# A decoder layer on one core: a new order in the opening of cross-attention, and routing with its place matmuls between wide ones

## What is computed

```
x = layernorm(x + self_attention(x))            # 32 heads of 16, causal
x = layernorm(x + cross_attention(x, context))  # 32 query heads, 8 key heads of 128, rotary
x = layernorm(x + experts(x) + shared(x))       # 16 experts of 256, the best 4 per token
scores = sigmoid(x @ gate_w.T) + bias           # the routing
topk_w, topk_idx = top_k(scores, 4)             # weights divided by their sum
out = sum over e of (silu(x Wg_e) * (x Wu_e)) * cw_e @ Wd_e + shared expert
```

## Time and profile before

| | us |
|---|---|
| median of 3 runs (1749.41 to 1754.07) | 1751.92 |
| the profiled execution | 1754.08 |
| its span | 1752.3 |
| TensorE busy | 1687.3 (96%) |
| VectorE busy | 1286.9 (73%) |
| ScalarE busy | 920.7 (53%) |
| GpSimd busy | 952.1 (54%) |

### The profile page before, as it was taken

How to read it: one execution, slowest core, us unless ns; L and a number is a source line. 1 busy time by engine, 2 the same in 40 slices (tenths; PEclk the granted TensorE clock), 3 DMA queues, 4 the chain that set the end, 5 groups by cost and what they waited for, 6 DMA issues and landing times. The chain is left out here.

```text
span 1752.3 us, 39049 instructions
## 1 busy us (share of the span) xinstructions
PE 1687.3 (96%) x15461; PEld 962.8 (55%) x15461; DVE 1286.9 (73%) x2062; ACT 920.7 (53%) x1518; POOL 952.1 (54%) x871
## 2 busy tenths in 40 slices
PE   7899999799999999999999999999889999999997
PEld 5666665455555555555555555555455555455553
DVE  6777777888888888888888888888785444344445
ACT  7676774656464645455555555565643333333334
POOL 5556664456464636465555556464634555455545
PEclk9999999999999999999999999999999999999999
DMA  5431323112212314132222132131267778877658
GB/s 164 132 86 35 79 62 81 61 57 89 69 65 73 109 43 145 44 101 93 73 74 97 37 98 71 37 109 37 82 224 217 143 147 224 242 189 150 117 97 300
DMA packets 88897, 190.68 MB, mean 109 GB/s; under 512 B 14800, under 2 KB 33744, under 8 KB 86672
## 3 DMA queue, kind: packets, MB, share of 16 engines
q1 hardware_dynamic: 65232, 130.72, 22.3%
q0 software_dynamic: 22912, 57.32, 16.1%
q10 hardware_dynamic: 576, 0.14, 0.0%
HBM read 124.95 MB, written 63.21 MB: 107 GB/s over the span
## 5 line engine op out<-in xcount | busy, mean ns | idle before, releaser
L1151 POOL TENSOR_TENSOR xa_sc<-xa_sc,xa_rs 128x1024 f32<-128x1024 f32 x32 | 60.8, 1901 | 366.4 <-DVE xa_rs L1415 366.4
L1139 POOL TENSOR_TENSOR xa_xs<-xa_xs,sn 128x512 f32<-128x512 f32 x160 | 227.8, 1424 | 52.1 <-ACT xa_xs L1221 52.1
L297 PE MATMUL bank<-xhl,front_h 128*128 128x512 f16 x640 | 244.7, 382 | 11.7 <-DVE front_l L679 9.8
L298 PE MATMUL bank<-xhl,front_h 128*128 128x512 f16 x640 | 244.5, 382 | 0.0
L299 PE MATMUL bank<-xhl,front_l 128*128 128x512 f16 x640 | 244.0, 381 | 0.0
L1146 POOL TENSOR_TENSOR xa_rr<-xa_x,xa_xs 128x512 f32<-128x512 f32 x156 | 232.0, 1487 | 17.9 <-DVE xa_x L1373 2.5
L297 PE MATMUL bank<-out_h,xa_oh 128*128 128x512 f16 x512 | 195.0, 381 | 12.9 <-DVE out_l L1418 5.2
L2195 POOL DMA_INDIRECT scratch_y<-raw_front,moe_to x79 | 125.3, 1585 | 149.8 <-DVE mo_zl L2249 118.6
L298 PE MATMUL bank<-out_l,xa_oh 128*128 128x512 f16 x512 | 194.7, 380 | 0.0
L299 PE MATMUL bank<-out_h,xa_ol 128*128 128x512 f16 x512 | 194.6, 380 | 0.0
L1220 ACT ACTIVATE xa_xs<-bank 64x512 f32<-64x512 f32 x160 | 95.0, 593 | 133.2 <-PE bank L299 117.7
(11 more groups left out here) (320 smaller groups left out, 4667.3 us busy)
## 6 DMA issues: line engine op xcount, KB each, us to landing
xa_rawc<-in_ew SPq DMA_DIRECT2D x32, 768.0 KB, 5.3
moe_ring<-scratch_w SPq DMA_DIRECT2D x16, 1536.0 KB, 8.8
scratch_w<-xa_chunk_h SPq DMA_DIRECT2D x32, 384.0 KB, 2.3
scratch_w<-xa_chunk_l SPq DMA_DIRECT2D x32, 384.0 KB, 3.3
raw_front<-in_xwq SPq DMA_DIRECT2D x8, 1024.0 KB, 7.9
raw_out<-in_xwo SPq DMA_DIRECT2D x8, 1024.0 KB, 5.8
scratch_y<-acc SPq DMA_DIRECT2D x6, 1024.0 KB, 6.3
acc<-in_x POOLq DMA_DIRECT2D x4, 1024.0 KB, 7.8
```

The source lines that it names most:

```text
L297: pe.matmul(out_ap, ah, bh, start=start and m == 0, stop=False)
L298: pe.matmul(out_ap, ah, bl, start=False, stop=False)
L1139: PO.mark(pool.tensor_tensor(xr, xr, sn[:, :].rearrange("p (a s) -> p a s", a=1) .to_broadcast([P, QT // S, S]), ALU.mult), f"sm{r}", st, ...
L1151: PO.mark(pool.tensor_tensor(s4, s4, rs[:, :, :].rearrange("p h (t a) -> p (h t) a", a=1) .to_broadcast([P, 16, S]), ALU.mult), "nm", st)
```

## The change

In the opening of cross-attention: on ScalarE the table of the exponential is loaded ahead by a one-element activation (`warm`), the first copies of step B and the exponentials of A go ahead of the norm. On VectorE the low parts of p go ahead of the second part of the output weights, the last part of these ahead of the low output parts, and the low half of the first chunk behind everything of step B's rotation. On TensorE the scores of step B's first half and the turned rows go ahead of the first two output tiles.

In routing: `at_col` is stored with its 83 columns innermost, so the moving operand is contiguous and VectorE's write has a step of 83 elements. w4 moves behind the fourth group, the products z1 behind `own`. The low parts zl1 are VectorE's instead of GpSimd's, behind `list`. TensorE does y0.0 and y0.1 ahead of the second half of `front(1)`; the 32 places of groups 0 to 3 stand one behind each of the 24 wide matmuls of that half, the other eight behind the last; those of groups 4 to 7 one behind each of the 12 wide matmuls of y0.2 and y0.3, the other 20 behind the last. `owners` follows. ScalarE's program in routing isn't changed, nor is SP's. The Timelines follow the programs; those of ScalarE, VectorE and TensorE that only mirror the order are left out here.

```diff
+                        act.activation(warm[:, :], eps[:, :], ACT.Exp)
+                        copies(b, 0)
+                        exponential(a, 0)
+                        copies(b, 1, ("woh",))
+                        exponential(a, 1)
                         ln.norm(act, 2, ln.DV, "sh2")
-                        exponential(a, 0)
-                        copies(b, 0)
-                        exponential(a, 1)
-                        copies(b, 1, ("woh",))
...
                         rotated_lo(b, 0)
+                        back_p_lo(b)
                         out_lo(1, 1)
-                        back_p_lo(b)
                         cosine(b, 2)
+                        rotated_lo(b, 1)
                         out_lo(2, 1)
-                        rotated_lo(b, 1)
-                        dve.wait_ge(AC.sem, AC.value("ch", a))
-                        chunk_lo().then_inc(s_first_l, 1)
                         cosine(b, 3)
                         rotated_lo(b, 2)
+                        DV.mark(out_lo(3, 1), "wol", b)
                         back_lo(b, (0, 1))
-                        DV.mark(out_lo(3, 1), "wol", b)
                         cosine(b, 4)
                         rotated_lo(b, 3)
                         back_lo(b, (2, 3))
                         value_lo(b)
                         rotated_lo(b, 4)
+                        dve.wait_ge(AC.sem, AC.value("ch", a))
+                        chunk_lo().then_inc(s_first_l, 1)
...
                         value(b, range(TQ))
+                        scores(b, 0)
+                        turned_rows(ln, b, 2)
                         back_out(b, (0, 1))
-                        turned_rows(ln, b, 2)
-                        scores(b, 0)
                         scores(b, 1)
                         back_out(b, (2, 3))
...
-            at_row, at_col = ([b(f"{w}{n}", [P, c, NR], F16) for n in range(NB)] for w, c in (("at_row", P), ("at_col", COLS)))
+            at_row = [b(f"at_row{n}", [P, P, NR], F16) for n in range(NB)]
+            at_col = [b(f"at_col{n}", [P, NR, COLS], F16) for n in range(NB)]
...
             DV = Timeline(sem("ro_dve"), [], 0,
-                          ["down", "chosen"] + quad("z", 0, IB) + ["w4", "slots"] + several("at", *range(4)) + quad("z", 1, IB)
-                          + several("at", *range(4, 8)) + ["own", "list", "tables", "to", "xl0", "xl1", "ws0", "ws1"])
-            PO = Timeline(sem("ro_pool"), [], 0, [x for q in range(2) for x in quad("zl", q, IB)])
+                          ["down", "chosen"] + quad("z", 0, IB) + ["slots"] + several("at", *range(4)) + ["w4"]
+                          + several("at", *range(4, 8)) + ["own"] + quad("z", 1, IB) + ["list"] + quad("zl", 1, IB) + ["tables", "to", "xl0", "xl1", "ws0", "ws1"])
+            PO = Timeline(sem("ro_pool"), [], 0, quad("zl", 0, IB))
...
-                low_parts(1)
...
-                        i = dve.tensor_tensor(at_col[g % NB][:, :, :], hit[g % 2][:, :, :], along(m.tok_no_h[:, ts], COLS), ALU.mult)
+                        i = dve.tensor_tensor(at_col[g % NB][:, :, :].rearrange("p n c -> p c n"), hit[g % 2][:, :, :], along(m.tok_no_h[:, ts], COLS), ALU.mult)
...
                 products(0)
-                then(dve.tensor_reduce(tot[:, :], top8[:, :, 0:TOPK], AX.X, ALU.add))
-                then(dve.tensor_scalar(tot[:, :], tot[:, :], 1e-20, None, ALU.add))
-                then(dve.reciprocal(rt[:, :], tot[:, :]))
-                DV.mark(dve.scalar_tensor_tensor(m.w4[:, :, :], top8[:, :, 0:TOPK], 1 / (WS * OS),
-                                                 rt[:, :].rearrange("p (t a) -> p t a", a=1).to_broadcast([P, NT, TOPK]),
-                                                 ALU.mult, ALU.mult), "w4", N0)
...
                 locate(0, 1, 2, 3)
-                products(1)
+                then(dve.tensor_reduce(tot[:, :], top8[:, :, 0:TOPK], AX.X, ALU.add))
+                then(dve.tensor_scalar(tot[:, :], tot[:, :], 1e-20, None, ALU.add))
+                then(dve.reciprocal(rt[:, :], tot[:, :]))
+                DV.mark(dve.scalar_tensor_tensor(m.w4[:, :, :], top8[:, :, 0:TOPK], 1 / (WS * OS),
+                                                 rt[:, :].rearrange("p (t a) -> p t a", a=1).to_broadcast([P, NT, TOPK]),
+                                                 ALU.mult, ALU.mult), "w4", N0)
                 locate(4, 5, 6, 7)
                 then(dve.tensor_scalar(past[:, :], end[:, :], m.tok_no[:, 0:1], None, ALU.is_lt))
                 then(dve.tensor_reduce(own_col[:, :], past[:, :], AX.X, ALU.add))
                 DV.mark(dve.tensor_scalar(own_h[:, :], own_col[:, :], float(NE - 1), None, ALU.min), "own", N0)
+                products(1)
                 wait(dve, PE, f"place{PLACES - 1}")
...
+                for n in range(IB):
+                    wait(dve, AC, f"zh1.{n}")
+                    DV.mark(dve.tensor_tensor(zl[1][:, n, :], z[:, n, :], zh[1][:, n, :], ALU.subtract), f"zl1.{n}", N0)
...
+                def place(g, n):
+                    if n == 0:
                         wait(pe, DV, f"at{g}")
+                    j, t = g * NR // NT, (g * NR + n) % NT
+                    mm = pe.matmul(bank[0][:, j * COLS:(j + 1) * COLS], at_row[g % NB][:, :, n], at_col[g % NB][:, n, :],
+                                   start=t == 0, stop=t == NT - 1, skip_group_check=True)
+                    if n == NR - 1:
                         PE.mark(mm, f"place{g}", N0)
 
...
+                def places(groups, first, last):
+                    for m in range(first, min(last, NR * len(groups))):
+                        place(groups[m // NR], m % NR)
+                def front_with_places(q, n, groups):
+                    wait(pe, DV, f"z{q - 1}.{n}")
+                    tok, m = slice(q * QT, (q + 1) * QT), 0
+                    for u in range(2):
+                        c, o = u * FI + n * P, bank[2 + 2 * n + u]
+                        for k in range(KD):
+                            h, l = wf_h[:, k, c:c + P], wf_l[:, k, c:c + P]
+                            for w, x in ((h, xh), (l, xh), (h, xl)):
+                                mm = pe.matmul(o[:, :], w, x[:, k, tok], start=k == 0 and w is h and x is xh,
+                                               stop=k == KD - 1 and x is xl, skip_group_check=True)
+                                m += 1
+                                if m == 6 * KD:
+                                    PE.mark(mm, f"gu{q}.{n}", N0)
+                                places(groups, m - 1, m)
+                    places(groups, m, 4 * NR)
+                def back(q, *ts, groups=()):
                     if q == 0:
                         wait(pe, DV, "down")
-                    wait(pe, PO, f"zl{q}.1")
+                    wait(pe, DV if q else PO, f"zl{q}.1")
+                    m = 0
                     for t in ts:
                         if t >= 2:
                             wait(pe, AC, f"y{q}.{t - 2}")
                         elif q:
                             wait(pe, AC, f"y{q - 1}.{t + 2}")
                         tok = slice(t * P, (t + 1) * P)
-                        PE.mark(three_pass(pe, bank[6 + t % 2][:, :], [(zh[q % 2][:, n, tok], zl[q % 2][:, n, tok], wo_h[:, n, :], wo_l[:, n, :])
-                                                                       for n in range(IB)]), f"y{q}.{t}", N0)
+                        for n in range(IB):
+                            for a, w in ((zh, wo_h), (zh, wo_l), (zl, wo_h)):
+                                mm = pe.matmul(bank[6 + t % 2][:, :], a[q % 2][:, n, tok], w[:, n, :], start=n == 0 and a is zh and w is wo_h,
+                                               stop=n == IB - 1 and a is zl, skip_group_check=True)
+                                m += 1
+                                if m % (3 * IB) == 0:
+                                    PE.mark(mm, f"y{q}.{t}", N0)
+                                places(groups, m - 1, m)
+                    places(groups, m, 4 * NR)
...
-                front(1)
-                place_picks(0, 1, 2, 3)
-                back(0, 0)
-                place_picks(4, 5, 6, 7)
+                front(1, 0)
+                back(0, 0, 1)
+                front_with_places(1, 1, range(4))
+                back(0, 2, 3, groups=range(4, 8))
                 wait(pe, DV, "own")
                 PE.mark(pe.matmul(bank[1][0:1, 0:NTILES + 2], own_h[:, :], identh[:, 0:NTILES + 2], start=True, stop=True), "owners", N0)
-                back(0, 1, 2, 3)
                 back(1, 0, 1)
```

38 lines of the change are left out of this document (15 added, 23 removed), and 2 rows, old and new, of the table opening.

## The result

The changed kernel takes 1774.03 us, median of four runs (1771.49 to 1777.36), beside 1751.88 us for the kernel before on the same chip (1749.41 to 1754.07): 22.1 us slower, a ratio of 1.0123 with a 95% interval of 1.0104 to 1.0142. The forecast was 12.5 us slower, 1764.4, with a range that ended at 1769. The sign was right, the size was not, and the range missed. One run of a later kernel (pairs and early copies, with the constant made early), 1960.15 us at a granted clock of 0.847 beside 0.99, is in a slower state of the chip and left out of that kernel's median.

A forecast was written before the change was run, and what follows sets the result against it. TensorE, 96% busy, was taken to bound the kernel. Opening -3.0, routing +15.0 and clock +0.5 gave +12.5 us: 1764.4 against the median; own range 1761 to 1768, outer ends 1755 and 1769.

The forecast's parts named there:

- The opening: Cross-attention's first steps: reordered engines shorten TensorE's holes, so step C begins earlier; 3.0 us gained, bounds 1 and 4.
- Step 2, the turned write: Routing, VectorE: at_col's strided write takes 1.3 us, bounds 0.42 and 1.4; a group 2.32 us, eight groups 18.6.
- Step 1: Routing, VectorE: w4's four operations leave the way, so the slots are done 0.9 us earlier, up to 1.9.
- Steps 3 and 4: Routing: w4 1.0, own 0.6, products 1.28 us behind the groups; TensorE idles some 12 us before y0.2.
- Step 5: Routing, TensorE: places cost 0.035 us between wide matmuls, 0.13 back to back; last place ends at 1343.5, against 1327.96.
- Step 6: Routing: last place to first turned rows takes 7.4 us, formerly 7.9; rows come at 1350.9, 15.0 us lost.
- The 0.5 for the clock behind the second hole: TensorE behind routing's second hole: 0.5 us lost to a lower clock.
- The plain rate: Rival in routing: at_col's write falls to one element a cycle, about 0.8 us; total 1760.1 us; chance 0.28.
- At_col at its old price: Rival in routing: at_col's write still costs 0.42 us, eight groups give 7.0 back; total 1757.4 us; chance 0.08.
- the opening that gives back 11 us: Rival in cross-attention's opening: all holes and half-clock stretches return, 11 us in all; total 1756.4 us; chance 0.08.
- No wait at y0.2: Rival in routing: products come before the copy of y0.0 is due, so TensorE doesn't wait; 1743.3 us; chance 0.06.

The follow-up runs named there:

- pairs and early copies, with the constant made early: Kernel after with at_col and hits laid out by column pairs, ScalarE's y0 copies ahead of zh1, pair constant made from early f32 counts: 1750.96 us (0.9983).
- The run that brought the group to 2.3 us by other means: Kernel after with at_col written column by column, eight two-scalar operations replacing hits and turned write: 1763.05 us, 1.0065 of the kernel before.
- The run with the copies early: Kernel after with ScalarE's copies of y0.0 and y0.1 ahead of zh1.0 and zh1.1, turned write kept: 1767.01 us, 1.0072 of the kernel before.

## Why the prediction was right and wrong

**The opening** (-3.0, bounds 1 and 4): right, if a little high: 2.1 and 2.2 us, by the medians of the two runs that have it alone. The hole ahead of the scores is 1.5 us, as worked out. The last low output weights ended at 331.64, the last cosine at 333.44, and the third step began at 348.44. Cross-attention itself started 1.1 us earlier than in the profile of before, so they are the 332.8, the 334.6 and, with the 0.7 us taken off for the clock, the 349.6 of the text, less that shift.

**Step 2, the turned write: this is the step that failed.** It took 1.3 us from L2014, "as the row that has the step", and 1.4 as the upper bound. It measures 2.54 to 2.6 from start to start. The row had a step, but an f32 output, and two-byte elements cost more than twice as much to write in steps (4.4 and 1.9 ns an element, measured side by side). Even the row as it stands, 0.73 us for 332 elements, is 2.2 ns each and gives 1.46 us for 664, above the upper bound; the text's 1.39 holds only if some 0.07 us of it is a fixed part, which it doesn't say. The text knew of the difference of type and used it as an argument for a cheaper write only; the upper bound was the same row once more, and so no bound. The eight groups take 29.9 us, 11.3 longer than in the sum. The run that brought the group to 2.3 us by other means bears out the mechanism: 12.3 us of wait, for about 12.

**Step 1**: the size was right, the reason not. By the stretch from the third step to the slots, moving w4 gains 1.2 us on average, for 0.9 (959.9 to 960.9 in the nine kernels with w4 behind and no late constant; 960.4 in the kernel before, 961.1 to 962.4 in the five others with w4 ahead); between the two profiles of before and after nothing of it shows. The slots were not held by GpSimd, as the text had it: L1972, the L1976 of before, takes its 0.42 us while GpSimd is at work until 1304.87.

```profile
1303.43 0.42 DVE L1972 TENSOR_TENSOR ro_prior<-moe_below,ro_till 128x256 f32<-128x256 f32 x1
1302.35 2.52 POOL L1851 TENSOR_TENSOR out_l<-raw_out,out_h 128x512 f16<-128x512 f32 x2 [9.76 <-ACT out_h L1871]
```

**Steps 3 and 4**: w4, "own" and the products measure 1.1, 0.7 and 1.3 against 1.0, 0.6 and 1.28, and the handover to TensorE 1.3 against 1.4. The wait is where it was named and for its reason: products behind eight groups, ScalarE's program untouched. The run with the copies early shows the waits for at_col that take its place, 7.0 us cheaper.

**Step 5**: the interleaved place costs 0.037 us, forecast 0.035. The 0.13 for places back to back was wrong: 0.06. I had laid the old price on the loading of at_row; it was the moving columns. at_row is read in steps in every kernel, and the price fell with at_col's layout alone. The Trainium skill, "SBUF — State Buffer", section "Door 1: The DMA port swizzle", says that accesses in the same line of 16 bytes run at full rate and that each one that goes to a new line pays. For the moving columns the runs agree: 83 of them in steps of 16 bytes take 0.15 us, in steps of 4 or 2 bytes 0.06. For the stationary at_row, also in steps of 16 bytes, they show no such price. From the restart to the last place it was 6.0 us instead of 8.3: 1.2 less for the 20 places at the end, 0.9 less for the twelve pairs ahead of them, since full clock was back after 3.3 us, and 0.2 by which the text's own 5.5 and 2.6 fall short of its 8.3.

**Step 6**: from the last place to the turned rows 5.4 us, not 7.4. Why the gather was faster than I allowed for, no run shows. The 0.5 for the clock behind the second hole didn't come up either: behind a hole of 1.9 us the matmuls of y1.0 and y1.1 are 0.22 us apart from 1351.89 on. Instead there are waits for the second tile's rows, and the stretch from the turned rows to the raw_out matmul is 0.9 us longer than before (8.2 and 7.2).

**The sum.** From the slots (ready at 1309.35) to the turned rows the text had 38.6 us, the trace has 45.7. The difference of 7.1 is 11.5 of groups, w4 and products, less 0.1 at the handover, 2.3 at the places and 2.0 at the gather. So two smaller errors, both the other way, hid part of the large one: that is luck. Against the profiled execution the forecast was 1766.6 and the measurement 1771.5; against the median the miss is 9.6, because the profiled execution of before was 2.2 us above its median and that of after 2.5 below.

**The rivals.** The plain rate (1760.1) lost: the write takes 2.9 us and not 0.8. The Trainium skill, "VectorE: DVE Perf Modes", section "What auto-detection actually checks", says that the doubled rate needs every tensor to be 16-bit with a step of 1 or -1. As far as that goes the trace agrees, since the operand repeated within the row takes the product from 0.50 to 0.85 us; of a write that takes 2.9 the section says nothing. At_col at its old price fell with the same row, and the opening that gives back 11 us with the 2.1 and 2.2 measured. No wait at y0.2 (1743.3) was far off: even with a cheap write and early copies the order of the change came to 1749.96 at best.

## What to carry to other kernels

Before turning a tile for one engine, ask in which order its writer can write it. A two-byte write in steps of 16 bytes or more cost six times the write in order here, and a pair of neighbours was enough to keep the writer at full rate and give TensorE its own. When an operation's price comes from a row, the type of the output must match as well as the pattern, and if it doesn't, the bound goes up and not only down. And where a change moves a producer back, look for engines whose program wasn't touched: 7 of the 24 us lay in two copies that stood behind the wrong operation.

## What the hardware showed that was not expected

- VectorE writes f16 in steps at 4.4 to 4.7 ns an element, whether the step is 8, 83, 84 or 128 elements, and f32 in steps of 83 at 1.9.
- TensorE loads a stationary operand of 128 by 128 in steps of 16 bytes without a visible cost: places take 0.037 us between wide matmuls and 0.06 back to back with it. The same step in the 83 moving columns costs 0.15.
- An f16 operation of 83 elements with two scalars takes 0.21 us from start to start, so eight of them take 1.78 us, more than three times the one of 664 elements in order.
- The same stage starts up to 6 us apart in profiles whose code ahead of it is the same. A median over runs evens it out, a comparison of two profiles doesn't: only stretches between rows can be compared.
